# Attention and FFN layer on eight cores: the attention output kept in f32, and its output projection in one f32 pass instead of three f16 passes

## The reference

```python
xn = _layernorm(x)
q, k, v = (proj(Wq), proj(Wk), proj(Wv))              # of xn, 16 heads of 64
scores = einsum('bhqd,bhkd->bhqk', q, k) * SCALE
w = sigmoid(scores)
w = w / (w.sum(axis=-1, keepdims=True) + 1e-6)
out = einsum('bhqk,bhkd->bhqd', w, v)
attn = einsum('bso,po->bsp', out, Wo)                 # the output projection
# FFN: 3 cycles of  out = out + coupling(out) * twist(out),
# coupling from a net 1024 -> 1024 -> 512 -> 256 -> 1 with GELU
return x + attn + ffn(xn)
```

## Time and profile before

| what | us |
|---|---|
| median of 2 runs (4167.69 to 4191.27) | 4179.48 |
| the profiled execution, its own time | 4217.19 |
| its span on the slowest core (core 6) | 4215.1 |
| TensorE busy in it | 3501.4 |
| ScalarE busy | 1092.4 |
| VectorE busy | 985.2 |

### The profile page before, as it was taken

One profiled execution on the slowest core, in us unless ns is written; L12 is line 12 of the kernel. 1 busy time (PEld: TensorE's weight loads), 2 busy tenths in 40 slices (PEclk: granted clock), 3 DMA queues, 4 the chain that ended last, 5 costly groups with the idle time before them and its releaser, 6 DMA issues.

```text
span 4215.1 us, 43547 instructions; the slowest of 8 cores (4160.4 to 4215.1 us)
## 1 busy us (share of the span) xinstructions
PE 3501.4 (83%) x14436; PEld 1779.3 (42%) x14436; DVE 985.2 (23%) x1619; ACT 1092.4 (26%) x2003; POOL 21.8 (1%) x8
## 2 busy tenths in 40 slices
PE   1487898898897898898898898887699999999995
PEld 0332232232232232232232232233577777777772
DVE  4322112212213112212212212212221111222224
ACT  3323323323323313323323323300121122222220
POOL 0000000000000000000000000001000000000000
PEclk9998789998998878999999999999898799999995
DMA  2000000000000000000000000000200000000004
GB/s 91 23 18 16 0 1 16 0 1 15 1 1 16 0 1 15 1 1 16 0 1 10 1 1 1 0 26 20 56 1 1 1 1 1 1 1 1 1 1 160
DMA packets 59918, 54.23 MB, mean 13 GB/s; under 512 B 2242, under 2 KB 53570, under 8 KB 59714
## 3 DMA queue, kind: packets, MB, share of 16 engines
q1 hardware_dynamic: 57410, 43.07, 3.5%
q10 hardware_dynamic: 2304, 8.39, 0.6%
HBM read 43.07 MB, written 8.39 MB: 12 GB/s over the span
## 4 chain that ended last, share of the span: by engine, by line
PE 78%; DVE 10%; ACT 5%; issue 4%; DMA 2%; DVEq 0%; ACTq 0%; SPq 0%
PE p L65 78%; DVE slotC L65 8%; ACT slotC L65 3%; DVE slotA L65 1%; ACT L65 1%; DMA wblk<-wvT 1%; DMA slotB<-x 1%; DVE wblk L65 0%; ACT slotA L65 0%; DMA wblk<-w 0%; DVE slotB L65 0%; ACT wblk L65 0%; ACT tf_sb L65 0%; DVEq L55 0%; DVE cp_sb L65 0%
## 5 line engine op out<-in xcount | busy, mean ns | idle before, releaser
L65 PE MATMUL p<-slotC 128*128 128x512 f16 (+1 forms) x4096 | 1523.5, 532 | 301.4 <-ACT slotC L65 283.4
L65 PEld LDWEIGHTS p<-slotC 128*128 128x128 f16 (+1 forms) x4096 | 503.5, 127 | 1338.3 <-issue 1189.1
L65 PE MATMUL p<-slotA 128*128 128x256 f16 (+1 forms) x6144 | 914.4, 314 | 53.2 <-DVE slotA L65 52.3
L65 PEld LDWEIGHTS p<-slotA 128*128 128x128 f16 (+1 forms) x6144 | 786.8, 129 | 183.1 <-issue 67.2
L65 ACT ACTIVATE slotC<-p 128x512 f32<-128x512 f32 x1024 | 603.9, 596 | 883.8 <-PE p L65 882.8
L65 PE MATMUL p<-slotA,slotC 128*128 128x512 f16 x2304 | 530.2, 394 | 5.0 <-DVE slotC L65 5.0
L65 PEld LDWEIGHTS p<-slotA,slotC 128*128 128x128 f16 x2304 | 230.1, 101 | 297.2 <-issue 88.0
L65 DVE TENSOR_SCALAR slotC<-p 1x512 f32<-1x512 f32 x64 | 43.8, 685 | 1284.3 <-PE p L65 1284.3
L65 PE MATMUL p<-identb,slotC 128*128 128x128 f32 x384 | 143.7, 398 | 205.1 <-ACT slotC L65 121.4
L65 DVE RECIPROCAL slotC<-p 64x512 f32<-64x512 f32 x64 | 214.4, 3350 | 90.8 <-PE p L65 90.1
L65 ACT ACTIVATE slotA<-p,cnb1b 128x256 f32<-128x256 f32 x192 | 90.9, 473 | 425.5 <-PE p L65 425.5
(11 more groups left out here) (56 smaller groups left out, 961.7 us busy)
## 6 DMA issues: line engine op xcount, KB each, us to landing
slotB<-x SPq DMA_DIRECT2D x1, 8192.0 KB, 29.8
slotA<-x ACTq DMA_DIRECT2D x16, 512.0 KB, 4.6
out<-slotA SPq DMA_DIRECT2D x16, 512.0 KB, 4.0
wblk<-wqT SPq DMA_DIRECT2D x8, 512.0 KB, 5.1
wblk<-wkT SPq DMA_DIRECT2D x8, 512.0 KB, 4.2
wblk<-wvT SPq DMA_DIRECT2D x8, 512.0 KB, 4.3
wblk<-woT SPq DMA_DIRECT2D x8, 512.0 KB, 4.1
wblk<-w SPq DMA_DIRECT2D x8, 512.0 KB, 4.2
```

Of the source, the lines that this page charges most:

```text
L65: return Inst(getattr(real, op)(*a, **k) if real is not None else None)
```

## The change

The normalised product is written into slotB as f32 by VectorE at once. `nprod`, ScalarE's copy and VectorE's subtraction are not used any more, and the reciprocal always uses partitions 0 to 63. The output projection loads its weight blocks through `load_block`, into wblk0 and wblk1 by turns, doesn't split them, and multiplies f32 with f32: one matmul instead of three.

```diff
-                        def mk_pending(b2=b2, n_sb=n_sb, dst_hi=dst_hi,
-                                       dst_lo=dst_lo, nx=next_mark, wvb=wvb,
-                                       hi_=hi_):
+                        def mk_pending(b2=b2, n_sb=n_sb, dst=dst, nx=next_mark,
+                                       wvb=wvb):
                             def pending():
                                 b3 = bacq(4)
                                 T.wait(sV, nx)
...
-                                V.reciprocal(recip[hi_ * 64:(hi_ + 1) * 64, 0:512],
-                                             b3[0:64, :]).inc(sV)
+                                V.reciprocal(recip[0:64, 0:512], b3[0:64, :]).inc(sV)
                                 bank_free[4] = [(sV, sV.n)]
-                                np_ = nprod[hi_ * 64:(hi_ + 1) * 64, 0:512]
-                                rc_ = recip[hi_ * 64:(hi_ + 1) * 64, 0:512]
                                 V.wait(sV)
-                                V.tensor_tensor(np_, b2[0:64, :], rc_,
+                                V.tensor_tensor(dst, b2[0:64, :], recip[0:64, 0:512],
                                                 ALU.mult).inc(sV)
                                 bank_free[wvb] = [(sV, sV.n)]
-                                Sc.wait(sV)
-                                Sc.copy(dst_hi, np_).inc(sS)
-                                V.wait(sS)
-                                V.tensor_tensor(dst_lo, np_, dst_hi,
-                                                ALU.subtract).inc(sV)
...
             for oc in range(NCH):
-                Y.waits(wblk_free[0])
-                ap = bass.AP(woT, oc * 128, [[1024, 128], [128 * 1024, 8], [1, 128]])
-                Y.dma_start(wblk0.ap().rearrange("p (kc o) -> p kc o", kc=8),
-                            ap).inc(swb[0], 16)
...
-                V.tensor_copy(woh[:, :], wblk0[:, 0:1024]).inc(sV)
-                V.wait(sV)
-                V.tensor_tensor(wol[:, :], wblk0[:, 0:1024], woh[:, :],
-                                ALU.subtract).inc(sV)
...
+                buf, ib, wready = load_block(woT, oc, 8, D)
                 for qc in range(NQT):
                     bi = 4 + qc % 2
                     b = bacq(bi)
-                    T.wait(sV, wsplit)
+                    T.waits([wready])
                     T.wait(sV, attn_V)
-                    passes = []
                     for kc in range(NCH):
...
-                        passes += [(lh, rh), (lh, rl), (ll, rh)]
...
+                        rhs = B[:, kc * S + qc * QT: kc * S + qc * QT + QT]
+                        inst = T.matmul(b[:, :], buf[:, kc * 128:(kc + 1) * 128], rhs,
+                                        start=(kc == 0), stop=(kc == NCH - 1))
```

More of the change, by code:

```diff
@@ L519, in emit @@
                                 pair * S + qc * QT: pair * S + qc * QT + QT]
[L521 to L525, removed]
-                        def mk_pending(b2=b2, n_sb=n_sb, dst_hi=dst_hi,
-                                       dst_lo=dst_lo, nx=next_mark, wvb=wvb,
-                                       hi_=hi_):
+                        dst = B[hi_ * 64: hi_ * 64 + 64,
+                                pair * S + qc * QT: pair * S + qc * QT + QT]
+                        def mk_pending(b2=b2, n_sb=n_sb, dst=dst, nx=next_mark,
+                                       wvb=wvb):
                             def pending():
@@ L561, in emit @@
                 tap_marks["attn"] = (tap_sems["attn"], 16)
-            w16v = wblk1.bitcast(F16)
-            woh, wol = w16v[:, 0:1024], w16v[:, 1024:2048]
             for oc in range(NCH):
-                Y.waits(wblk_free[0])
-                ap = bass.AP(woT, oc * 128, [[1024, 128], [128 * 1024, 8], [1, 128]])
-                Y.dma_start(wblk0.ap().rearrange("p (kc o) -> p kc o", kc=8),
-                            ap).inc(swb[0], 16)
-                wready = (swb[0], swb[0].n)
-                V.waits([wready])
-                V.wait(sT)
-                V.tensor_copy(woh[:, :], wblk0[:, 0:1024]).inc(sV)
-                V.wait(sV)
-                V.tensor_tensor(wol[:, :], wblk0[:, 0:1024], woh[:, :],
-                                ALU.subtract).inc(sV)
-                wblk_free[0] = [(sV, sV.n)]
-                wsplit = sV.n
+                buf, ib, wready = load_block(woT, oc, 8, D)
                 for qc in range(NQT):
@@ L581, in emit @@
                     b = bacq(bi)
-                    T.wait(sV, wsplit)
+                    T.waits([wready])
                     T.wait(sV, attn_V)
-                    passes = []
                     for kc in range(NCH):
[L586 to L590, removed]
-                        passes += [(lh, rh), (lh, rl), (ll, rh)]
[L592 to L596, removed]
+                        rhs = B[:, kc * S + qc * QT: kc * S + qc * QT + QT]
+                        inst = T.matmul(b[:, :], buf[:, kc * 128:(kc + 1) * 128], rhs,
+                                        start=(kc == 0), stop=(kc == NCH - 1))
+                        if kc == NCH - 1:
                             inst.inc(sT)
@@ L601, in emit @@
                     bank_free[bi] = [(sS, sS.n)]
-            wblk_free[1] = [(sT, sT.n)]
+                wblk_free[ib] = [(sT, sT.n)]
             wo_T, wo_S = sT.n, sS.n
```

## The result

| | kernel before, us | changed kernel, us |
|---|---|---|
| median of all executions | 4359.9 (10; 4167.7 to 4738.3) | 3945.2 (11; 3780.5 to 4303.2) |
| ratio, with its 95% interval | | 0.908 (0.889 to 0.926) |
| the same, measured again, 6 executions (the last run of experiment 8) | | 3758.4; 0.902 (0.897 to 0.907) |
| predicted | | 3750 (3700 to 3890); ratio 0.897 |

Both kernels have executions in which TensorE's clock is held at 0.81 on some cores for hundreds of us; the ratios compare executions that are nearly free of that, the medians of the first line do not. The changed kernel is 9 to 10% faster, near the 10% forecast, but its median of 3945 lies above the stated range.

A forecast was written before the change was run, and what follows sets the result against it. TensorE sets the time, stalled at chunk boundaries by ScalarE's CAST waiting for VectorE. Saving 458 us there, less 28 for the output projection, nets -430: 3750 us from the median of 4179.5; range 3700 to 3890.

The forecast's parts named there:

- 458 forecast: Attention's 63 chunk boundaries: total saving from removing the CAST and subtract, 458 us, bounds 283 and 476.
- 49 ordinary: Ordinary chunk boundaries in attention: stall and slow stretch removed, 6.59 us each, 323 us.
- 7 with splits: Boundaries where the next pair's weight splits precede the reciprocal on VectorE: 14.7 us saved each, 103 us.
- 7 behind a projection: Boundaries after projections, where TensorE starts at the slow clock: 4.5 us saved each, 2.6 still lost, 32 us.
- Together 22.1 us: Steady attention chunk without the stall, from one ones-matmul to the next: 22.1 us, against 28.69 measured before.
- The steps of 1.29, the 0.97 and the 0.51: Parts of a steady chunk: sixteen key-tile steps, ones-matmul until the next matmul, wait for `n_sb`, in us.
- +28 us: Output projection: 256 f32 matmuls at 0.86 us, 220 us, plus 2 for slow start; stage ends 28 us later.
- from the median I get 3750: Final step: 430 us net saving applied to the kernel before's median of 4179.5 us, giving 3750, 10% less.
- rival A: Denser work holds TensorE's clock at 0.81: attention +333 us, output projection +51; chances 0.07 part, 0.02 attention, 0.02 everywhere.
- B: Chunk boundaries: the stall goes but the clock still drops, 158 us back, 3908 us; chance 0.03.
- C: Output projection: f32 weight loads of 128 columns don't hide, +110 us, 3860 us; chance 0.04.
- D: Chunk boundaries: another equally long wait replaces the stall, 4207 us, no change; chance 0.02.

The follow-up runs named there:

- experiment 8: Changed kernel rerun unaltered (4121.6 us; last run 3758.4), and both kernels with normalised input zeroed (changed 3756.1 to 3757.5, before 4150.5 to 4155.3).
- Experiments 1 and 3: 1: changed kernel plus only ScalarE's wait for VectorE's product, 4264.7 us; 3: kernel before with CAST and subtract emitted behind key tile 12, 3730.9 us.
- experiment 4: Kernel before with only the output projection made f32, ScalarE still copying the product at the old place in its queue; 4183.9 us.
- experiment 5: Kernel before with late CAST (behind key tile 12), plus two alternating buffers for the output projection's split weights; 3706.6 us, ratio 0.893 to the kernel before.

## Why the prediction was right or wrong

**The mechanism: right.** ScalarE's CAST between two sigmoids made TensorE wait for the reciprocal. Experiments 1 and 3 show it from both sides: the wait alone brings 368 of 422 us back, and the work alone, at another place, costs nothing in a chunk.

**The size.** Between the first and the last reciprocal, in two undisturbed profiles (kernel before with zeros, changed kernel), 2369.2 us became 1952.0: 417 saved, 458 forecast. By kind, from the distances of the ones-matmuls:

| kind | forecast each | measured each | sum |
|---|---|---|---|
| 49 ordinary | 6.59 | 28.7 - 22.5 = 6.2 | 303 for 323 |
| 7 with splits | 14.7 | 35.7 - 22.5 = 13.1 | 92 for 103 |
| 7 behind a projection | 4.5 | 29.0 - 25.7 = 3.3 | 23 for 32 |

The term that was mis-sized is "Together 22.1 us", too low by 0.4 (63 x 0.4 = 25 us). The steps of 1.29, the 0.97 and the 0.51 are all in the new rows as they were read, but the piece between two ones-matmuls is 21.04 and not 16 x 1.29 = 20.64. A chunk's end isn't a step as the others: its last product has no scores between it and its sigmoid. That this makes the 0.4 is argued from the order of the instructions; no run tries it alone. The slow start behind a projection lasted about 6 us (windows of 1 us at 0.50 to 0.54 from 1056 to 1063), not 5. The one chunk with splits that was read, 36.8, was a long one: they are 35.7 on average.

**The output projection: right.** Forecast 0.86 us for an f32 matmul, 2 for the slow start and +28 us; measured 0.858, so 219.7 of the 222.48, 2.8 for the slow start, and +28 in experiment 4. Its weight loads hide.

**The net.** Undisturbed, 4152 became 3757: 395 us for 430, ratio 0.905 for 0.897. The terms above give 417 - 28 = 389; the other 6 are not traced, about what undisturbed executions differ by.

**What failed** is the step "from the median I get 3750". It took a median of two executions, 4179.5, as the kernel's time. Both happened to be little disturbed. In the four later sets of the kernel before, 40 executions, only 14 had no held core, and their medians are 4239 to 4520, that is 2 to 9% above the undisturbed 4152; those of the changed kernel, 3758 to 4122, are 0 to 10% above 3757. The step also had its warning beside it: the profiled execution's slowest core had been held, and rival A priced a hold of the attention at 333 us. But A was weighed as something that the change might call forth, at 0.07 in part and 0.04 in full, where it is there in both kernels. The forecast of 3750 misses 3945 by 5%. Where no core is held it is met (3755 to 3759), but by luck: the base was 28 us too high (4179.5 for 4152) and the saving 35 too large (430 for 395), and the two errors cancel.

**The rivals.** B (the clock falls at each boundary still): not so, one piece of 21.04 us at full clock. C (weight loads don't hide): not so. D (another wait): not so, 2.5 us of idle. A: the level exists and costs what was said (chunks of 27.0 in a held stretch of core 6, 27.3 forecast), but the kernel before has it too; whether the change makes it a little more or less frequent stays open.

## What to carry to other kernels

In a queue that runs in order, look for an instruction that waits for a long chain on another engine and stands ahead of one that the bottleneck needs next; moving it behind some later steps gave here all that removing it gave, and let the cheaper f16 passes stay. Price a stall of TensorE twice, by its idle time and by the half clock behind it: cutting it from 3.75 to 1.38 us saved the difference of the first and all of the second. Where cores of a chip are held at times, compare undisturbed cores or run once on zeros, take more than two executions as the base, and give a median of all executions a range that holds both kinds.

## What the runs showed of the hardware

- The hold at 0.81 follows the data: 0 of 136 cores in 17 executions on zeros, 124 of 320 in 40 executions of the kernel before on real data. It comes to some cores of a chip and not to others in the same execution, lasts from tens of us to some 2,000 us (core 2 in experiment 8), and ends under the same load.
- A stall of TensorE of 1.38 us left the clock at 1.00; of seven gaps of 2.38 us three were followed by a stretch at 0.50 and four not (experiment 5); stalls of 3.75 to 3.96 us were followed by one in each boundary looked at.
- An f32 matmul of 512 columns takes 0.858 us at full clock with 128 weight columns and some 0.86 with 65: the number of weight columns doesn't show.
- Undisturbed executions of the kernel before agree within 5 us (4150.4 to 4155.3) on four chips.
